# A recommendation model on one core: GpSimd's gathers wait for the landing of the gather two places back instead of TensorE's transposes

## The reference

```python
h = relu(dense_x @ bw1 + bb1)                     # 512 x 256
x_bottom = relu(h @ bw2 + bb2)                    # 512 x 128
sparse_embs = emb_tables[field_idx, sparse_x]     # 512 x 26 x 128, out of range indices wrapped and clamped
combined = concatenate([x_bottom[:, None, :], sparse_embs], axis=1)   # 512 x 27 x 128
interactions = einsum('bfd,bgd->bfg', combined, combined)             # 512 x 27 x 27
x_int = interactions[:, rows, cols]               # the 351 pairs f < g
x_final = concatenate([x_bottom, x_int], axis=-1)
t = relu(x_final @ tw1 + tb1)                     # 128
t = relu(t @ tw2 + tb2)                           # 64
return sigmoid(t @ tw3 + tb3)                     # 512 x 1
```

## Time and profile before

| what | value |
|---|---|
| time, median of 3 runs | 173.94 us (173.8 to 174.83) |
| the profiled execution's own time | 174.63 us |
| its span in the trace | 172.8 us |
| mean granted clock of TensorE | 0.752 of full |
| busy: TensorE matmuls / weight loads | 105.5 us (61%) / 82.2 us (48%) |
| busy: VectorE / ScalarE / GpSimd | 56.4 us (33%) / 39.4 us (23%) / 98.5 us (57%) |
| DMA, mean over the span | 45 GB/s, the gathers 15.2% of 16 engines |

### The profile page before, as it was taken

The page is one execution under the profiler, slowest core; times in us unless marked ns, Lnnn a source line. Parts: engine busy times, 40 slices in busy tenths (PEclk is TensorE's granted clock), DMA queues, the critical chain, the costliest instruction groups (busy, mean ns, idle before and its releaser), DMA issues.

```text
span 172.8 us, 1457 instructions
## 1 busy us (share of the span) xinstructions
PE 105.5 (61%) x448; PEld 82.2 (48%) x448; DVE 56.4 (33%) x219; ACT 39.4 (23%) x145; POOL 98.5 (57%) x108
## 2 busy tenths in 40 slices
PE   3976771877359349709676368519460981644863
PEld 1325541765149238609466255319350861543661
DVE  2511106620453015156314026176105260426330
ACT  3320003400422015044013024044004060314132
POOL 1777772777467737737775557737772776620000
PEclk9999999999999955895555559855855598555558
DMA  5212120122111211211121111202121121110000
GB/s 163 81 46 61 46 61 15 46 58 52 47 30 48 58 30 49 56 35 46 49 61 46 46 28 47 51 25 61 46 65 30 40 53 46 46 30 0 0 0 0
DMA packets 3795, 7.76 MB, mean 45 GB/s; under 512 B 1854, under 2 KB 1854, under 8 KB 3788
## 3 DMA queue, kind: packets, MB, share of 16 engines
q0 software_dynamic: 3328, 6.82, 15.2%
q1 hardware_dynamic: 434, 0.82, 1.5%
q10 hardware_dynamic: 26, 0.04, 0.1%
HBM read 7.67 MB, written 0.00 MB: 44 GB/s over the span
## 4 chain that ended last, share of the span: by engine, by line
another core or an unknown queue 48%; PE 18%; ACT 13%; DVE 10%; issue 8%; DMA 1%; DVEq 0%
ACT pairs L166 11%; PE products L342 8%; DVE pairs L166 7%; PE top_ps L357 4%; DVE fields L225 3%; PE rows_T L306 2%; PE products L311 2%; PE top_ps L366 1%; DMA db<-dense_bw 1%; ACT top L272 1%; ACT fields L261 1%; PE rows_T L325 1%; ACT probs L284 0%; PE top_ps L372 0%
## 5 line engine op out<-in xcount | busy, mean ns | idle before, releaser
L190 POOL DMA_INDIRECT rows<-table,row_index x104 | 98.2, 945 | 55.2 <-issue 28.1
L342 PE MATMUL products<-fields 128*128 128x104 f32 x256 | 55.1, 386 | 23.0 <-DVE fields L225 22.7
L342 PEld LDWEIGHTS products<-fields 128*128 128x128 f32 x256 | 51.0, 295 | 27.9 <-DVE fields L225 26.1
L166 ACT COPY pairs<-products 32x56 f32<-32x56 f32 (+1 forms) x128 | 31.1, 243 | 95.8 <-remote 67.2
L166 DVE COPY pairs<-products 32x56 f32<-32x56 f32 (+1 forms) x128 | 30.9, 241 | 52.8 <-remote 35.5
L325 PE MATMUL rows_T<-w,rows 128*128 128x128 f32 x104 | 33.8, 400 | 20.9 <-DMA rows<-table,row_index 20.1
L225 DVE COPY fields<-rows_T 128x494 f32<-128x494 f32 (+6 forms) x83 | 21.9, 319 | 52.8 <-remote 27.0
L325 PEld LDWEIGHTS rows_T<-w,rows 128*128 128x128 f32 x104 | 19.5, 200 | 32.4 <-DMA rows<-table,row_index 29.5
L357 PE MATMUL top_ps<-pairs,wp 128*128 128x128 f32 x56 | 12.6, 415 | 8.0 <-ACT pairs L166 4.8
L357 PEld LDWEIGHTS top_ps<-pairs,wp 128*128 128x128 f32 x56 | 11.9, 321 | 8.8 <-issue 8.8
L366 PE MATMUL top_ps<-top,w 128*64 128x128 f32 x8 | 2.5, 411 | 10.2 <-ACT top L272 10.2
(11 more groups left out here) (14 smaller groups left out, 7.7 us busy)
## 6 DMA issues: line engine op xcount, KB each, us to landing
rows<-table,row_index POOLq DMA_INDIRECT x104, 2.6
wp<-pair_weights SPq DMA_DIRECT2D x1, 448.0 KB, 3.7
w<-weights SPq DMA_DIRECT2D x1, 291.5 KB
raw<-index_base SPq DMA_DIRECT2D x1, 58.5 KB, 2.1
db<-dense_bw ACTq DMA_DIRECT2D x1, 39.0 KB
out<-probs SPq DMA_DIRECT2D x1, 2.0 KB
```

The costliest lines, as they stand in the source:

```text
L166: last = copy(dst[SLOT * j:SLOT * (j + 1), h, s, 0:g1 - g0], src[SLOT * s:SLOT * (s + 1), s, g0:g1])
L190: nc.gpsimd.indirect_dma_start(rows[:, c, :], None, table, bass.IndirectOffsetOnAxis(row_index[:, group, k:k + 1], 0)).then_inc(gathered[c ...
L342: ins = nc.tensor.matmul(products[h][:, col:col + n], four, four[:, :, 1:1 + SPARSE], start=True, stop=True)
```

## The change

GpSimd loses its waits for `transposed` and with them the tie to TensorE's progress. In front of each gather from the third on it now waits until the gather two places back has landed (`gathered[c - 2]` at 16). So at most two gathers are under way at a time, and otherwise GpSimd issues to the end of the 104 without regard to the other engines. Their programs are as they were.

```diff
-LEAD = 5
+IN_FLIGHT = 2
...
         @block.gpsimd
         def _(pool):
-            unit_ends = [g * GROUP_CHUNKS + c1 for g in range(GROUPS) for _, c1 in units_of(g)]
             for c in range(GROUPS * GROUP_CHUNKS):
                 group, k = divmod(c, GROUP_CHUNKS)
                 if c < 2:
                     pool.wait_ge(index_ready, c + 1)
-                if c - LEAD in unit_ends:
-                    pool.wait_ge(transposed, unit_ends.index(c - LEAD) + 1)
+                if c >= IN_FLIGHT:
+                    pool.wait_ge(gathered[c - IN_FLIGHT], 16)
                 nc.gpsimd.indirect_dma_start(
                     rows[:, c, :], None, table,
                     bass.IndirectOffsetOnAxis(row_index[:, group, k:k + 1], 0)
                 ).then_inc(gathered[c], 16)
```

## The result

The changed kernel took 203.87 us (median of 4 runs, 199.72 to 209.59), the kernel before beside it 174.38 us (4 runs, 173.8 to 175.57). Without the two runs of the changed kernel that lie more than 1.5% above its fastest, the ratio is 1.151, 95% interval 1.135 to 1.167, so slower by 15%; with them it is 1.169. The profiled execution shown here took 205.74 us with a span of 203.9, 0.9% above the median.

The account below looks back on a forecast made before the run. TensorE's late signals were taken as the bound. Last gather at 151.0, landing 2.6 and transpose 0.45 give 154.05; plus 11.8 gives span 165.85, as a time 167.7, on the median's scale 167.0 us; range 161.8 to 185.

Parts of the forecast that it names:

- What bounds the kernel: Step naming the bound: TensorE's signals arriving 5.8 and 7.4 us after its last instruction, not any engine's work.
- late signals: TensorE's semaphore signals reaching waiting engines 5.8 and 7.4 us after its last instruction, though nobody is busy in between.
- Removed: GpSimd's waits for `transposed`: of 23.2 us, 20.2 us leave its row; nothing else depends on them.
- Added: 102 GpSimd waits for the landing two back: always bind, period 1.43 us, last gather at 151.0 against 152.96.
- no gap over about 0.9 us: Sign expected in GpSimd's row of the changed profile, with gathers in pairs of 1.25 and 1.6 us.
- Moved: Behind the gather stream: TensorE keeps up if signals are on time; last transposes end at 154.05, plus 11.8, span 165.85.
- Rival A: Slower: signals come through when GpSimd stops, so without pauses they stay late; 183.6 us, some 190 throughout; chance 0.35.
- The point from which it decides: Gather period below about 1.45 us, at which the slower rival, that the pauses were the cure, would decide.
- Rival B: No change: gathers and TensorE's signals share one used-up capacity, so lateness only shifts; 172 to 176 us; chance 0.17.
- Rival C: Faster still: the landing wait never binds, period 1.25 us, end at 147.5, time 149 us; chance 0.03.
- The chances: Weights given: forecast 0.45, Rival A 0.35, Rival B 0.17, Rival C 0.03; faster 0.48, same 0.17, slower 0.35.
- seven bursts: GpSimd's gather stream, cut by ten waits: 1.43 to 1.46 us for each gather from restart to restart, however long the burst.

Follow-up runs that it names:

- on-time place: Sets of runs in which the kernel before took 149 to 152 us; whether chip or moment decides is not known.
- two memsets: Changed kernel without its landing waits, two memsets of 64 numbers a partition behind each gather: 208.27 us, ratio 1.20.
- both waits: Kernel before with the wait for the landing two back added to its `transposed` waits: 174.72 us against 174.05, ratio 1.004.
- the even 1.455: Changed kernel without its landing waits, four memsets of 40 numbers a partition behind each gather: 169.66, 170.25 and 170.51 us.
- late place: Sets of runs (the result's and the first follow-up set) in which the kernel before took 173 to 176 us.
- wide products: Changed kernel with each unit's four product matmuls replaced by one four times as wide: 162.52, 161.77, 161.32 and 162.07 us.
- half rows: Changed kernel with gathers of 64 of each row's 128 numbers (32 KB), the rest zeroed once: 158.29, 159.38 and 158.77 us.

## Why the prediction was wrong

It forecast 167.0 us, faster by 4%; the time was 203.87, slower by 15%, above the range's upper end of 185.

- **What bounds the kernel: right for this place.** The late signals bound the kernel before, and they bound the changed one. But I took them for a property of the program. The same program ran at 150 us with no late signal, where its bound is the 1.25 us that a gather takes on GpSimd.
- **"Removed": right for GpSimd's row**, which the 20.2 us of waits left. "Nothing else depends on those waits" was true of the tile `rows` only: with them TensorE's signals are on time, without them up to 28 us late.
- **"Added": right.** The period was to be 1.43, between 1.38 and 1.48, and came out at 1.405; the last gather was to start at 151.0 (145.9 to 156.1), and started at 148.40. The landings of the earlier trace rows were a thinner basis than I took them for: "the shortest landing of 104" was the shortest of three. That the range of 1.38 to 1.48 held is partly luck; the on-time traces with all 104 landings have 2.4 to 3.3 us, median 2.5. The sign "no gap over about 0.9 us" did not hold: the gap in front of the last gather is 1.54. The estimate of a 2.15 us landing from the Trainium skill ("DMA: Bandwidth & Descriptors", section "Anatomy of one DMA"), by which the waits would never bind, is contradicted by every trace: the shortest landing of a 64 KB gather on record is 2.4, and at the on-time place the landings were the chain.
- **"Moved": here it failed.** "If the signals are on time at the slower, even pace, TensorE keeps up" was the condition of the whole sum, and it did not hold. From the last gather to the end it was to be 165.85 - 151.0 = 14.85 us and was 203.9 - 148.40 = 55.5. Where the condition held, at the on-time place, the same stretch took 160.5 - 146.30 = 14.2 us, so the arithmetic of the step was sound and its premise was not.
- **Rival A, "the pauses were the cure", named the sign and the signals rightly, and was priced too low.** It gave 183.6, to 190 at worst (these are spans; as times they are 1.8 us longer), because it took groups of 22 to 24 us, read from a kernel that still had pauses. Without them the groups took 21.5, 53.3 and 46.5 us, and only 2 groups more, with a third 1.4 us later, were through at the last landing instead of 5.5. After it the groups were faster than the 13.8 us that I took (10.5 us on average), since they waited for no landings. Shown: with the `transposed` waits put back, 174.72; without any wait, 223.59. Not shown: that it is the pauses that cure. The waits also slow the mean to 1.503 us, and without any pause some signals do get through. Its working, "behind by 0.02 to 0.07 us with each gather", was far too small: the lateness is no sum of such pieces. A signal seen 2 us late at 41 us and one due at 115 us and 22 us late came at the same pace of gathers.
- **The point from which it decides**, a period below 1.45, is not contradicted: even periods of 1.387 (landing wait) and 1.36 (two memsets, both medians) were late, a median of 1.453 with both waits was on time. It is not shown either, since "both waits" also has pauses, and the even 1.455 never ran at the late place.
- **Rival B** gave 172 to 176 and did not come. Its mechanism, one capacity for gathers and signals, stays open, since the runs that could have tested it (wide products, half rows) all fell on the on-time place. **Rival C** is refuted: the wait bound 66 times at the late place and 98 times at the on-time place.
- **The chances.** "Signals come through when GpSimd stops" and "a steady pace is enough" were both read from the same seven bursts, whose pace and whose pauses can't be told apart. I gave the second one more weight although the rows that I named for the first were the more direct ones, and the even pace of the change, 1.43 or less, was on the wrong side of my own 1.45.

What stays open: what the lateness is made of (number of gathers, their bytes, TensorE's instructions), what sets a late place apart from an on-time one, and whether it exists in an unrecorded run. That the change is the slower one holds at both places. No version tried was clearly faster than the kernel before in its own set.

## What to carry to other kernels

When the chain runs through semaphore events without a sender, first run the unchanged kernel again elsewhere: if it comes out at another time, the trace shows the place as much as the program, and an edit should be judged at both. A wait that looks like a loss may be what keeps another engine's signals in time; before it is removed, keep it and add the new one beside it, which here would have shown at once that the old one carried some 29 us. Before a duration is taken from a profile, count from how many instances it comes: here it was 3 of 104. And a limit on transfers in flight costs the distance between landing and issue: with two in flight, half of (landing + wake), here 1.38 to 1.41 us against 1.25, times every gather.

## What of the hardware was unexpected

- The same program has two times, 174 and 150 us, by the set in which it ran; with no wait on GpSimd 223.6 and 150.0.
- At the late place TensorE's semaphore increments reached the other engines up to 61 us after the instruction that makes them, while TensorE itself went on seeing landings, and VectorE's and ScalarE's increments were recorded within 0.01 us of their last instruction. In the changed kernel nothing was late once the last gather had landed; with no wait at all signals stayed late for some 14 us more.
- With them records went missing, down to 261 of 1664 steps, and with memsets between the gathers GpSimd was held back by up to 1.5 us between two instructions without a wait.
- GpSimd's gather of 128 rows took 0.94 to 0.95 us, with 0.30 us of gap where nothing stood between two; two memsets of 64 numbers a partition between them moved the period from 1.25 to 1.36 us. Halving the bytes of a gather shortened its landing by 0.1 us only, from 2.5 to 2.4 (medians of 104 each).
